# The edge counts of a tensor-product layer, with the one-hots as moving data

## The chip, the cores and the metric

The kernel runs on one core of a Trainium2 chip. The metric is the time of one execution on the device in microseconds. The core has five engines that work side by side: TensorE (matrix products, PE in the profile, its loads of weights PEld), VectorE (DVE), ScalarE (ACT), GpSimd (POOL) and SyncE (SP). Semaphores order their work against each other.

## The reference

Four graph layers run one after the other on 3125 nodes of 256 values and 100000 edges. Each layer's result is added to the nodes and normalized. The change is in the second, a tensor-product layer (`_L1_gnn_ref`). What matters of it:

```python
h = silu(edge_attr @ fc_w1 * ...)
h = silu(h @ fc_w2 * ...)
w = h @ fc_w3 * ...
wA, wB, wC, wD = split(w, 4, axis=1)
...
ns = segment_sum(mid_s, src, num_segments=N)
nv = segment_sum(mid_v, src, num_segments=N)
deg = segment_sum(ones((src.shape[0],)), src, num_segments=N)
dn = rsqrt(maximum(deg, 1.0))
ns = ns * dn[:, None]
nv = nv * dn[:, None, None]
```

So the layer sums 512 values per edge (`mid_s` and `mid_v`) at the edge's source node, counts the edges of each node (`deg`), and scales each node's sums by one over the root of its count.

## The kernel before, in words

**Order of the edges.** At its start the kernel sorts the edges by bucket, once by destination and once by source. A bucket is 128 consecutive nodes; there are NB = 26 (the last one is for padding). The sorted edges are worked on in macros of ME = 512 edges, as Q = 4 quarters of 128 edges, one edge per partition. All edges of a macro belong to one bucket. `jmap_s` has one entry per macro: its bucket j.

**One turn.** The layer has NM = 224 turns. Each engine runs its own loop over them, written out by hand for U = 4 turns (`macro_loops`), and meets the others at semaphores alone. A turn with M(0) as the macro to be summed does:
- GpSimd (`pool_a`) gathers the rows of `y` for macro M(3), SyncE (`sync_a`) loads its records.
- TensorE (`tensor`, `turn`) goes through two macros by turns. For M(2) it computes the edge weights `w`: `transposes` (L1796), `layer_1` (L1802), `layer_2` (L1809), `layer_3` (L1817). Between them it does the four quarters of `sums` (L1827, L1828) for M(0): quarter 0 after the transpose, quarter 1 after `layer_1`, quarters 2 and 3 after `layer_2`.
- ScalarE (`act`) applies silu and copies for M(2), among them L1856, which makes `layer_1`'s operand, and, first in its turn, L1866 for the macro before.
- VectorE writes the one-hots (`one_hot`) of M(3) and the messages of M(1) (`messages`), then adds the finished sums of M(0) (`add_sums`, L1911 and L1912).

**The sums.** The one-hot `oh[:, u, q, :]` of a quarter has a row per edge and a column per node of the bucket. L1828 loads it as weights (128x128, f32) and streams the 512 values of the messages through it, in two passes of the profile, into bank 5 or 6 of PSUM. L1827 loads the upper halves of the same one-hot as bf16 weights and streams one column of ones, which gives the counts of this bucket's nodes in one column, in bank 2 or 7. Both pairs of banks alternate from turn to turn, so a turn waits for the flush of two turns before. At the end of a turn L1911 adds that column to column j of `deg` in SBUF, and L1912 adds the 512 columns to `acc[:, j]`. Both read j into a register of VectorE.

**After the loop.** `scale` (VectorE) takes the larger of `deg` and 1, `root` (ScalarE) its square root, and `scale` the reciprocal. `deg` has nodes on partitions and buckets in columns.

**Names used below.** The attention layers use similar loops. In the last one (L1373 to L1429) L1400 is a bf16 matmul with 24 columns of weights (`turn_scores`), L1410 and L1413 have 128 columns of weights (`node_scores`), and L1373 reads j into a register of TensorE. In the first, L962 is a transpose to 8 rows and L989 a matmul with 128x128 weights.

Of the kernel before, what the change touches and what calls it, by code (L numbers as in the profile page):

```python
# [16 lines left out]
I32 = mybir.dt.int32  # L17
BF16 = mybir.dt.bfloat16
ALU = mybir.AluOpType
# [3 lines left out]
P = 128  # L23
# [12 lines left out]
NB = NT + 1  # L36
PAD_KEY = NB * P - 1
Q = 4
# [4 lines left out]
NMA = NM + 6  # L43
# [50 lines left out]
def top(ap):  # L94

    return ap.bitcast(BF16)[..., 1::2]
# [6 lines left out]
def gnn_kernel(nc, io, out):  # L103
    ctx = ExitStack()
    with ctx:
        def sb(name, shape, dt=F32):
            return ctx.enter_context(nc.sbuf_tensor(name, shape, dt))

        def sem(name):
            return ctx.enter_context(nc.semaphore(name))  # L110
# [17 lines left out]
        ident = sb("ident", [P, P])  # L128
        ones = sb("ones", [P, P])
# [5 lines left out]
        jmap = {"d": sb("jmap_d", [1, NMA], I32), "s": sb("jmap_s", [1, NMA], I32)}  # L135
        deg = sb("deg", [P, NB])
# [4 lines left out]
        oh = sb("oh", [P, U, Q, P])  # L141
# [3 lines left out]
        small = sb("small", [P, 640])  # L145
        wts = sb("wts", [P, 3 * 2 * D])
        rows = sb("rows", [P, 3 * D])
        by_src = sb("by_src", [P, 3, EC + EC // (NM // U)])

        ps = ctx.enter_context(nc.psum_tensor("ps", [P, 8, 512], F32))  # L150
# [4 lines left out]
        def S(name):  # L155
            if name not in sems:
                sems[name] = sem(name)
            return sems[name]

        T = nc.tensor  # L160
        V = nc.vector
# [6 lines left out]
        def vchain(e):  # L168

            the_vchain.e = e  # L170
            return the_vchain
# [4 lines left out]
        def phase(**fns):  # L176

            bars[0] += 1
            meet = 5 * bars[0]
            for name, todo in programs.items():  # L180
                todo.append((fns.get(name), meet))
# [406 lines left out]
        def both(*fns):  # L588
            return lambda e: [fn(e) for fn in fns]

        phase(sync=both(load, project0["sync"]), vector=both(place, project0["vector"]),
              tensor=both(totals, project0["tensor"]), scalar=fill_ring, gpsimd=scatter)
# [195 lines left out]
        def macro_loops(ahead, first, body, after=None, start=0, side=None):  # L788

            def go(e):
                for m in range(ahead):
                    first(e, Macro(0, m))
                if side and side[0]:
                    side[0](e)
                for m in range(start):
                    body(e, lambda lag, m=m: Macro(0, m + lag))
                with e.Fori(0, NM // U) as i:
                    for u in range(U):  # L800
                        body(e, lambda lag, i=i, u=u + start: Macro(i, u + lag))
                        if side:
                            side[1](e, i, u)
                if side and side[2]:
                    side[2](e)
                if after:
                    after(e)
            return go
# [896 lines left out]
        def layer1():  # L1705
# [36 lines left out]
            s = stages("e1", "oh", "tr", "at", "h1", "g1", "h2", "g2", "w", "wac", "wr", "msg", "sum", "flush")  # L1742
# [16 lines left out]
            msg = [big[:, u * 2048:(u + 1) * 2048].rearrange("p (q c h n) -> p q c h n", q=Q, c=4, h=2)  # L1759
                   for u in range(2)]  # L1760
            psW = ps[:, 3:5, :].rearrange("p b c -> p (b c)").rearrange("p (q k n) -> p q k n", q=Q, k=4)
            psDeg = [ps[:, 2, 0:1], ps[:, 7, 0:1]]
            acc = acc_raw[:, :, 0:2 * D]

            def sync_a(e, m):
                i = e.snap(m.index())
# [52 lines left out]
                                        start=True, stop=True)  # L1819
                last.then_inc(s["w"], 1)  # L1820

            def sums(e, m, q):
                if q == 0:
                    e.wait_ge(s["oh"], m.done())
                    e.wait_ge(s["msg"], m.done())
                    e.wait_ge(s["flush"], m.done(2))
                T.matmul(psDeg[m.v], top(oh[:, m.u, q, :]), top(ones[:, 0:1]), start=(q == 0), stop=(q == Q - 1))  # L1827
                ins = T.matmul(ps[:, 5 + m.v, :], oh[:, m.u, q, :],  # L1828
                               msg[m.v][:, q].rearrange("p c h n -> p (c h n)"),
                               start=(q == 0), stop=(q == Q - 1))  # L1830
                if q == Q - 1:
                    ins.then_inc(s["sum"], 1)

            def tensor(e):
                e.wait_ge(S("e1_fc"), 16 * (Q + 4))
                e.wait_ge(S("e1_go"), 1)
                for m in range(2):
                    for part in (transposes, layer_1, layer_2, layer_3):
                        part(e, Macro(0, m))

                def turn(e, M):

                    transposes(e, M(2))
                    sums(e, M(0), 0)
                    layer_1(e, M(2))
                    sums(e, M(0), 1)
                    layer_2(e, M(2))
                    sums(e, M(0), 2)
                    sums(e, M(0), 3)
                    layer_3(e, M(2))  # L1850
                macro_loops(0, None, turn)(e)

            def act(e, m):
                e.wait_ge(s["tr"], m.done())
# [51 lines left out]
            def add_sums(c, e, m):  # L1906
                j = e.value_load(jmap["s"][0:1, bass.ds(m.index(), 1)], min_val=0, max_val=NB - 1)
                e.wait_ge(s["flush"], m.done(1))
                e.wait_ge(s["sum"], m.done())
                dj, aj = deg[:, bass.ds(j, 1)], acc[:, bass.ds(j, 1), :]  # L1910
                V.tensor_tensor(dj, dj, psDeg[m.v], ALU.add)  # L1911
                V.tensor_tensor(aj, aj, ps[:, 5 + m.v, :], ALU.add).then_inc(s["flush"], 1)  # L1912

            def dve(e):
                c = vchain(e)
                c(V.memset(deg[:, :], 0.0))
                c(V.memset(rows[:, 0:384], 0.0))
                c.wait()
                e.sem_inc(S("e1_go"), 1)
                for m in range(2):  # L1920
                    for q in range(Q):
                        one_hot(e, Macro(0, m), q)
                cc = Chain(e, cB)
                messages(cc, e, Macro(0, 0), Macro(0, 2))
                per = cc.n
                e.wait_ge(S("zeroed"), 1)

                def turn(e, M):
                    c = Chain(e, cB)
                    c.n = per * M(1).off  # L1930
                    c.enter(M(1).i, U * per)
                    messages(c, e, M(1), M(3))
                    assert c.n - c.at == per
                    add_sums(c, e, M(0))
                macro_loops(0, None, turn)(e)

            def pool(e):
# [4 lines left out]
                  scalar=macro_loops(2, act, lambda e, M: act(e, M(2))), tensor=tensor, vector=dve)  # L1942
# [9 lines left out]

            def scale(e):
                c = vchain(e)
                c(V.tensor_scalar(deg[:, :], deg[:, :], 1.0, None, ALU.max))
                c.wait()
                e.sem_inc(s_act[0], 1)
                e.wait_ge(s_act[1], 1)
                c(V.reciprocal(dn, deg[:, :]))
                c.wait()  # L1960
# [2 lines left out]
                e.wait_ge(s_act[0], 1)  # L1963
                A.activation(deg[:, :], deg[:, :], ACT.Sqrt).then_inc(s_act[1], 1)

            phase(vector=scale, scalar=root)


            out_scale = (2 * MUL) ** -0.5 * MUL ** -0.5
# [253 lines left out]
```

## Time and profile before

| | us |
|---|---|
| median of 3 runs | 9040.61 (9038.01 to 9045.36) |
| the profiled execution | 9037.91 |
| its span in the trace | 9036.1 |
| TensorE busy with matmuls | 6249.3 (69%) |
| VectorE busy | 5729.5 (63%) |
| GpSimd busy | 6125.2 (68%) |
| ScalarE busy | 2476.3 (27%) |
| matmuls L1828, 1792 passes | 960.7 |
| gathers L1787 | 1218.7 |

The tensor-product layer's loop runs from about 3620 to 5108 us of the span. Busy time counts the records of instructions. A matmul's record contains the way through the array too, so records of neighbouring matmuls overlap, and a busy TensorE isn't one at its peak. The profile shows for each group of instructions how long the engine was idle ahead of it and what ended that. The granted clock of TensorE has two levels, 0.5 (1.2 GHz) and 1.0 (2.4 GHz); in between a stretch is a mixture. Names with q behind them (PEldq) are an engine's sequencer.

### The profile page before, as it was taken

To read this page: it belongs to the slowest core of one execution; us is meant where nothing else is said; L and a number is where in the kernel's file an instruction comes from. 1 tells how busy PE (TensorE), PEld (TensorE's weight loads), DVE (VectorE), ACT (ScalarE), POOL (GpSimd) and SP (SyncE) were. 2 spreads that over 40 slices of the span, in tenths; PEclk is the share of its full clock that TensorE was granted. 3 is DMA by queue.
4 is the path that set the end of the run, shared out by engine and by line. 5 is a ranking of instruction groups with operands and counts; after the bars stand their busy time and mean duration, and the time that the engine had idled before them with its cause. 6 is when DMAs were issued, how large, how long until landed. Compare 5 with 4: busy or idle time off the path is not lost. (4 is left out here: it accounts for less than half of the span.)

```text
span 9036.1 us, 124148 instructions
## 1 busy us (share of the span) xinstructions
PE 6249.3 (69%) x27682; PEld 3822.4 (42%) x27683; DVE 5729.5 (63%) x14736; ACT 2476.3 (27%) x7366; POOL 6125.2 (68%) x5632
## 2 busy tenths in 40 slices
PE   5100077777777775999999778888888887555554
PEld 2000044444444444444444445555555555334433
DVE  7000076666666665888888778888888887322223
ACT  0000044444444442333333223333333333000000
POOL 4777677777777774888888635555555555677772
PEclk8555577777777777999999889999999998777776
DMA  2000043333343342333233533333333344333354
GB/s 88 13 1 1 8 117 104 107 106 106 107 108 108 108 106 60 86 84 85 84 85 85 53 94 105 105 105 105 105 105 106 105 106 92 98 104 104 105 99 50
DMA packets 411759, 790.73 MB, mean 88 GB/s; under 512 B 198754, under 2 KB 228172, under 8 KB 411084
## 3 DMA queue, kind: packets, MB, share of 16 engines
q0 software_dynamic: 283584, 725.19, 31.8%
q1 hardware_dynamic: 128140, 65.15, 2.5%
q8 instruction: 13, 0.21, 0.0%
q14 instruction: 22, 0.18, 0.0%
HBM read 749.73 MB, written 40.22 MB: 87 GB/s over the span
## 5 line engine op out<-in xcount | busy, mean ns | idle before, releaser
L1787 POOL DMA_INDIRECT gat<-y,rec_sb_s x908 | 1218.7, 1342 | 276.5 <-issue 259.4
L1545 DVE TENSOR_REDUCE small<-ps 128x2 f32<-128x1024 f32 x900 | 1091.7, 1222 | 308.1 <-PE ps L1413 266.4
L907 POOL DMA_INDIRECT gat<-kv,rec_sb_d x912 | 988.3, 1084 | 302.1 <-issue 275.2
L1350 POOL DMA_INDIRECT gat<-kv,rec_sb_s x916 | 889.9, 971 | 403.6 <-issue 314.3
L2051 POOL DMA_INDIRECT gat<-x,rec_sb_d x908 | 863.1, 951 | 332.2 <-issue 265.0
L2065 PE MATMUL ps<-gat,oh 128*128 128x256 f32 x1792 | 664.4, 537 | 528.7 <-DMA gat<-x,rec_sb_d 402.5
L495 POOL DMA_INDIRECT rec_s<-wts,rows x784 | 836.5, 1067 | 238.9 <-issue 238.3
L434 POOL DMA_INDIRECT rec_d<-small x784 | 764.9, 976 | 335.2 <-issue 247.2
L1828 PE MATMUL ps<-big,oh 128*128 128x512 f32 x1792 | 960.7, 635 | 0.0
L1360 POOL TENSOR_TENSOR big<-gat,big 128x1024 f32<-128x1024 f32 x225 | 442.6, 1967 | 588.4 <-ACT big L1483 588.4
L989 PE MATMUL ps<-big,oh 128*128 128x264 f32 x1800 | 795.3, 558 | 0.4
L939 PE MATMUL ps<-qz,work 128*128 x1824 | 672.6, 533 | 145.1 <-issue 135.7
L2065 PEld LDWEIGHTS ps<-gat,oh 128*128 128x128 f32 x1792 | 458.6, 268 | 734.3 <-issue 390.0
L928 PE MATMUL ps<-work,oh 128*128 128x128 bf16 x912 | 119.6, 272 | 883.4 <-DVE oh L1096 883.2
L2085 DVE TENSOR_TENSOR acc<-acc,ps 128x256 f32 x224 | 94.3, 421 | 826.1 <-PE ps L2065 826.1
L1410 PE MATMUL ps<-wts,work 128*128 128x512 bf16 x1804 | 613.0, 425 | 0.0
L1413 PE MATMUL ps<-wts,small 128*128 128x512 bf16 x1804 | 608.9, 423 | 0.0
L1217 DVE TENSOR_TENSOR big<-ps,gat 128x1024 f32<-128x1024 f32 x226 | 276.7, 1224 | 480.9 <-DMA gat<-kv,rec_sb_d 480.3
L939 PEld LDWEIGHTS ps<-qz,work 128*128 128x128 f32 x1824 | 463.9, 267 | 248.2 <-issue 164.0
L1241 DVE MEMSET acc<- 128x6864 f32 x1 | 5.8, 5778 | 868.3 <-issue 868.3
L1040 ACT ACTIVATE work<-ps 128x512 f32<-128x512 bf16 x228 | 136.1, 597 | 1353.1 <-PE ps L928 1353.1
L928 PEld LDWEIGHTS ps<-work,oh 128*128 128x128 bf16 x912 | 84.1, 123 | 973.8 <-issue 937.4
(276 smaller groups left out, 13812.2 us busy)
## 6 DMA issues: line engine op xcount, KB each, us to landing
gat<-kv,rec_sb_s POOLq DMA_INDIRECT x916
gat<-kv,rec_sb_d POOLq DMA_INDIRECT x912
rec_sb_s<-rec_s SPq DMA_DIRECT2D x456, 32.0 KB, 1.8
gat<-y,rec_sb_s POOLq DMA_INDIRECT x908
gat<-x,rec_sb_d POOLq DMA_INDIRECT x908
kv<-big SPq DMA_DIRECT2D x52, 256.0 KB, 2.0
rec_d<-small POOLq DMA_INDIRECT x784
rec_s<-wts,rows POOLq DMA_INDIRECT x784
```

The lines of the kernel that those rows point to most:

```text
L434: e.indirect_dma_start(out=recs["d"], out_offset=bass.IndirectOffsetOnAxis(ap=pring[:, h * RH + t:h * RH + t + 1], axis=0), in_=rr[:, h, t ...
L495: e.indirect_dma_start(out=recs["s"], out_offset=bass.IndirectOffsetOnAxis(ap=pr[:, t:t + 1], axis=0), in_=rr[:, t, :], in_offset=None).th ...
L907: e.indirect_dma_start(out=gat[:, m.u, q, :], out_offset=None, in_=table, in_offset=bass.IndirectOffsetOnAxis(ap=r_sb[:, m.u, q, 0:1].bitc ...
L939: last = T.matmul(to, oht[:, m.v, q * P:(q + 1) * P], qz[:, bass.ds(j, 1), :], start=True, stop=True)
L989: last = T.matmul(psO[m.v], oh[:, m.u, q, :], pvb[:, m.v, q, :], start=(q == 0), stop=(q == Q - 1))
L1350: e.indirect_dma_start(out=gat[:, m.u, q, :], out_offset=None, in_=table, in_offset=bass.IndirectOffsetOnAxis(ap=r_sb[:, m.u, q, 0:1].bitc ...
L1410: T.matmul(to[:, n, :], bigI, nh[m.u], start=True, stop=False)
L1545: V.tensor_reduce(mx[:, 2 * pair:2 * pair + 2], psH[pair % 2], AX.X, ALU.max).then_inc(s_hr, 1)
L1787: e.indirect_dma_start(out=rows_y[m.u][:, q, :], out_offset=None, in_=y1, in_offset=bass.IndirectOffsetOnAxis(ap=r_sb[:, m.u, q, 0:1].bitc ...
L1828: ins = T.matmul(ps[:, 5 + m.v, :], oh[:, m.u, q, :], msg[m.v][:, q].rearrange("p c h n -> p (c h n)"), start=(q == 0), stop=(q == Q - 1))
L2051: e.indirect_dma_start(out=gat[:, m.u, q, 0:D], out_offset=None, in_=x3, in_offset=bass.IndirectOffsetOnAxis(ap=r_sb[:, m.u, q, 0:1].bitca ...
L2065: last = T.matmul(ps[:, 5 + m.v, 0:D], oh[:, m.u, q, :], gat[:, m.u, q, 0:D], start=(q == 0), stop=(q == Q - 1))
```

## The change

The counting matmul has its operands exchanged. `row_of` is a strip of 51 or 52 bf16 columns that are zero but for a one in column 25 (NB - 1). Its slice from column r on, 26 wide, has a one in row position 25 - r only. With the slice from j' = 25 - j as weights and the one-hot as 128 moving columns, the matmul adds the quarter's counts in row j of a 26x128 block of PSUM and zeros in the other rows. That block, in bank 2, is opened with zeros ahead of the loop, accumulates over all 224 turns, and is closed behind it. So nothing is added to `deg` in a turn. TensorE needs j' for each macro: `row_at` holds it for all of them (`V.tensor_scalar` from `jmap_s`), and each turn begins with a register load of it on TensorE (`row_start`). After the loop the block has buckets on partitions, so VectorE copies it, TensorE transposes it, and `scale` goes on from PSUM.

```diff
-            psDeg = [ps[:, 2, 0:1], ps[:, 7, 0:1]]
+            psDeg = ps[0:NB, 2, 0:P]
+            row_of = small[:, 336:362].bitcast(BF16)
             acc = acc_raw[:, :, 0:2 * D]
+            zero_row = small[:, 384:512]
+            counts = small[0:NB, 512:640]
+            row_at = by_src[0:1, 0, 0:NMA].bitcast(I32)
...
-            def sums(e, m, q):
+            def row_start(e, m):
+                return e.value_load(row_at[0:1, bass.ds(m.index(), 1)], min_val=0, max_val=NB - 1)
+
+            def sums(e, m, q, j):
...
-                T.matmul(psDeg[m.v], top(oh[:, m.u, q, :]), top(ones[:, 0:1]), start=(q == 0), stop=(q == Q - 1))
+                T.matmul(psDeg, row_of[:, bass.ds(j, NB)], top(oh[:, m.u, q, :]), start=False, stop=False)
...
+                T.matmul(psDeg, row_of[:, 0:NB], top(zero_row), start=True, stop=False)
+
                 def turn(e, M):
-
+                    j = row_start(e, M(0))
                     transposes(e, M(2))
-                    sums(e, M(0), 0)
+                    sums(e, M(0), 0, j)
...
                 macro_loops(0, None, turn)(e)
+                T.matmul(psDeg, row_of[:, 0:NB], top(zero_row), start=False, stop=True)
...
-                dj, aj = deg[:, bass.ds(j, 1)], acc[:, bass.ds(j, 1), :]
-                V.tensor_tensor(dj, dj, psDeg[m.v], ALU.add)
+                aj = acc[:, bass.ds(j, 1), :]
                 V.tensor_tensor(aj, aj, ps[:, 5 + m.v, :], ALU.add).then_inc(s["flush"], 1)
...
-                c(V.memset(deg[:, :], 0.0))
+                c(V.memset(row_of, 0.0))
+                c(V.memset(zero_row, 0.0))
                 c(V.memset(rows[:, 0:384], 0.0))
+                c.wait()
+                c(V.memset(row_of[:, NB - 1:NB], 1.0))
+                c(V.tensor_scalar(row_at, jmap["s"][:, :], -1.0, float(NB - 1), ALU.mult, ALU.add))
...
-                c(V.tensor_scalar(deg[:, :], deg[:, :], 1.0, None, ALU.max))
+                c(V.tensor_copy(counts, psDeg))
+                c.wait()
+                e.sem_inc(S("o1_counts"), 1)
+                e.wait_ge(S("o1_turned"), 1)
+                c(V.tensor_scalar(deg[:, :], ps[:, 0, 0:NB], 1.0, None, ALU.max))
...
+            def turn_counts(e):
+                e.wait_ge(S("o1_counts"), 1)
+                T.transpose(ps[:, 0, 0:NB], counts, ident[0:NB, 0:NB]).then_inc(S("o1_turned"), 1)
+
+            phase(vector=scale, scalar=root, tensor=turn_counts)
```

On TensorE, one turn of the layer's loop, before: the transpose, the quarters of the sums and the layers of M(2). A row's last number pair is the output (rows of the array x columns that move).

```order
L1796 MATMUL ps<-ident,rec_sb_s 64x128 [waits e1_rec3,e1_g2]
L1826 REGISTER_ALU [waits e1_msg,e1_oh]
L1827 MATMUL ps<-ones,oh 128x1 [waits e1_flush]
L1828 MATMUL ps<-big,oh 128x512
L1799 REGISTER_ALU
L1802 MATMUL ps<-work,rows 128x128 [waits e1_g1,e1_at]
L1802 MATMUL ps<-work,rows 128x128
L1827 MATMUL ps<-ones,oh 128x1
L1828 MATMUL ps<-big,oh 128x512
L1809 MATMUL ps<-work,rows 128x256 [waits e1_g1,e1_g2]
```

The same place after (L1796, L1802, L1809, L1827, L1828 have become L1800, L1806, L1813, L1834, L1835):

```order
L1827 ISA
L1827 TENSOR_LOAD by_src
L1827 ISA x2
L1800 MATMUL ps<-ident,rec_sb_s 64x128 [waits e1_rec3,e1_g2]
L1833 REGISTER_ALU [waits e1_msg,e1_oh]
L1834 ISA [waits e1_flush]
L1834 MATMUL ps<-oh,small 26x128
L1835 MATMUL ps<-big,oh 128x512
L1803 REGISTER_ALU
L1806 MATMUL ps<-work,rows 128x128 [waits e1_g1,e1_at]
L1806 MATMUL ps<-work,rows 128x128
L1834 MATMUL ps<-oh,small 26x128
```

No matmul has moved: each counting matmul stands where it stood, with 26 rows and 128 columns in place of 128 rows and one column. New are the register load with its three register operations ahead of the turn, and one register operation ahead of the first counting matmul, which now carries the wait for the flush.

On VectorE, the end of a turn, before:

```order
L1907 ISA
L1907 TENSOR_LOAD jmap_s
L1907 ISA x2
L1911 ISA [waits e1_sum,e1_flush]
L1911 TENSOR_TENSOR deg<-deg,ps 128x1
L1912 ISA
L1912 TENSOR_TENSOR acc<-acc,ps 128x512
```

and after:

```order
L1917 ISA
L1917 TENSOR_LOAD jmap_s
L1917 ISA x2
L1921 ISA [waits e1_sum,e1_flush]
L1921 TENSOR_TENSOR acc<-acc,ps 128x512
```

One operation of one column and its register operation are gone; the wait for the sums now stands ahead of the addition of 512 columns.

The last attention loop isn't changed. On TensorE its register load of j (L1373) stands in the program as follows:

```order
L1410 MATMUL ps<-wts,work 128x512 [waits a2_hr,a2_sp]
L1410 MATMUL ps<-wts,work 128x512
L1413 MATMUL ps<-wts,small 128x512 x2
L1410 MATMUL ps<-wts,work 128x512 [waits a2_hr]
L1410 MATMUL ps<-wts,work 128x512
L1413 MATMUL ps<-wts,small 128x512 x2
L1373 TENSOR_LOAD jmap_s
L1373 ISA x2
```

The load is the last of these in the program and stands there before and after alike.

## Rows read from the trace of the kernel before

**Rows 1.** The page, busy us (share of the span) and instructions of each engine.
```profile
PE 6249.3 (69%) x27682; PEld 3822.4 (42%) x27683; DVE 5729.5 (63%) x14736; ACT 2476.3 (27%) x7366; POOL 6125.2 (68%) x5632
```
**Rows 2.** Table by stretches: us, busy PE, PEld, DVE, ACT, POOL, clock, DMA share, GB/s.
```profile
4300.00:4600.00 300.00, 291.67 (x1231) 142.46 (x1231) 267.11 (x638) 93.38 (x320) 244.53 (x183) 1.00 0.30 84
```
**Rows 3.** Waits, 3700 to 5000 us: waiting line, releaser, us in total, times, longest.
```profile
PE ps L1802 <- ACT work L1856: 35.7, 197, 0.2
DVE deg L1911 <- PE ps L1828: 142.0, 196, 0.8
```
**Rows 4.** Timeline of one turn: start, us, engine, line, operation, output and inputs.
```profile
4307.67 0.30 PE L1796 MATMUL ps<-ident,rec_sb_s 128*64 128x128 f32 x1
4307.81 0.17 PE L1827 MATMUL ps<-ones,oh 128*128 128x1 bf16 x1
4307.84 1.10 PE L1828 MATMUL ps<-big,oh 128*128 128x512 f32 x2
...
4308.80 0.27 ACT L1856 ACTIVATE work<-ps 64x128 f32<-64x128 f32 x1
...
4309.12 0.71 PE L1802 MATMUL ps<-work,rows 64*128 64x128 f32 x4 [0.18 <-ACT work L1856]
...
4311.84 0.94 DVE L1903 TENSOR_TENSOR big<-work,rec_sb_s 128x768 f32<-128x768 f32 x1
```
**Rows 5.** Single lines: durations in ns (min/median/max), first and last start.
```profile
L1827 PE MATMUL ps<-ones,oh x788: 166/167/179, 3700.4 to 4998.8; 128*128 128x1 bf16 x197
...
L1828 PE MATMUL ps<-big,oh x1576: 592/634/677, 3700.4 to 4999.3; 128*128 128x512 f32 x197
...
L1802 PE MATMUL ps<-work,rows x788: 271/272/374, 3701.7 to 4996.2; 64*128 64x128 f32 x197
...
L1400 PE MATMUL ps<-work,small x904: 218/219/228, 5328.1 to 7629.0; 128*24 128x128 bf16 x181
...
L1911 DVE TENSOR_TENSOR deg<-deg,ps x224: 139/155/156, 3633.4 to 5107.3; 128x1 f32 x112
```
**Rows 6.** Timeline, TensorE, from quarter 2 to quarter 3 of the sums.
```profile
4311.18 0.17 PE L1827 MATMUL ps<-ones,oh 128*128 128x1 bf16 x1
...
4312.15 0.17 PE L1827 MATMUL ps<-ones,oh 128*128 128x1 bf16 x1
4312.17 0.68 PE L1828 MATMUL ps<-big,oh 128*128 128x512 f32 x1
```
**Rows 7.** Timeline, TensorE, last attention loop, around L1400.
```profile
5600.93 0.38 PE L1413 MATMUL ps<-wts,small 128*128 128x512 bf16 x1
5601.24 0.39 PE L1400 MATMUL ps<-work,small 128*24 128x128 bf16 x4
5601.57 0.39 PE L1410 MATMUL ps<-wts,work 128*128 128x512 bf16 x1
```
**Rows 8.** Timeline, TensorE, from L1802 to quarter 1 of the sums.
```profile
4316.16 0.27 PE L1802 MATMUL ps<-work,rows 64*128 64x128 f32 x1
4316.36 0.18 PE L1827 MATMUL ps<-ones,oh 128*128 128x1 bf16 x1
```
**Rows 9.** Timeline, TensorE, first attention loop, around L962.
```profile
1173.90 0.27 PE L962 MATMUL ps<-ident,small 128*8 128x128 f32 x1 [1.06 <-DVE small L1150]
1174.01 0.45 PE L989 MATMUL ps<-big,oh 128*128 128x264 f32 x1
```
**Rows 10.** Line L1373 on TensorE's sequencer, 5646.5 to 5647.4 us.
```profile
L1373 PEldq TENSOR_LOAD <-jmap_s x1: 297/297/297, 5646.6 to 5646.6; - x1
L1373 PEldq SEQ_ASSERT  x1: 18/18/18, 5647.2 to 5647.2; - x1
```
**Rows 11.** Timeline, TensorE, the same stretch.
```profile
5647.31 0.63 PE L1413 MATMUL ps<-wts,small 128*128 128x512 bf16 x1
```
**Rows 12.** Line L1794 on TensorE's sequencer, 4310 to 4318 us.
```profile
L1794 PEldq FUSED_REGOPS  x1: 43/43/43, 4312.5 to 4312.5; - x1
```
**Rows 13.** Timeline, TensorE, the transpose behind L1794.
```profile
4314.27 0.30 PE L1796 MATMUL ps<-ident,rec_sb_s 128*64 128x128 f32 x1
```

More of the change, by code:

```diff
@@ L1839, in tensor @@
                         part(e, Macro(0, m))
+                T.matmul(psDeg, row_of[:, 0:NB], top(zero_row), start=True, stop=False)
                 def turn(e, M):
+                    j = row_start(e, M(0))
                     transposes(e, M(2))
-                    sums(e, M(0), 0)
+                    sums(e, M(0), 0, j)
                     layer_1(e, M(2))
-                    sums(e, M(0), 1)
+                    sums(e, M(0), 1, j)
                     layer_2(e, M(2))
-                    sums(e, M(0), 2)
-                    sums(e, M(0), 3)
+                    sums(e, M(0), 2, j)
+                    sums(e, M(0), 3, j)
                     layer_3(e, M(2))
                 macro_loops(0, None, turn)(e)
+                T.matmul(psDeg, row_of[:, 0:NB], top(zero_row), start=False, stop=True)
             def act(e, m):
@@ L1964, in root @@
                 A.activation(deg[:, :], deg[:, :], ACT.Sqrt).then_inc(s_act[1], 1)
-            phase(vector=scale, scalar=root)
+            def turn_counts(e):
+                e.wait_ge(S("o1_counts"), 1)
+                T.transpose(ps[:, 0, 0:NB], counts, ident[0:NB, 0:NB]).then_inc(S("o1_turned"), 1)
+            phase(vector=scale, scalar=root, tensor=turn_counts)
             out_scale = (2 * MUL) ** -0.5 * MUL ** -0.5
```

## The prediction

> **What bounds the kernel now.** Start with the page's busy shares [rows 1]. No engine is full over the whole span (TensorE 69%, VectorE 63%), so a share of the span decides nothing. The change touches only the tensor-product layer, so take the table by stretches there [rows 2]: in 300 us of it TensorE has 291.7 us of matmuls, VectorE 267, GpSimd 245, ScalarE 93, at the full granted clock (1.00, which is 2.4 GHz). The table of waits counts 197 turns in 1300 us [rows 3], so a turn takes 6.60 us.
>
> Which wait ends last is read from the same table [rows 3]. TensorE waits for another engine at one line only, L1802 for ScalarE's L1856, 35.7 us in 197 turns, 0.18 us each. VectorE waits for TensorE's sums ahead of L1911, 142.0 us in 196 turns, 0.72 us each: it is early. So a turn is two pieces, and the timeline of one turn shows them [rows 4]. Once the turn before has done its L1817, ScalarE makes the four copies of L1866 and then L1856, until 4309.07, and TensorE beside it does L1796 and the first quarter of the sums (L1827, L1828), then waits. From L1802 at 4309.12 to the end of L1817 TensorE runs alone and decides. A cost on TensorE counts in full in the second piece (quarters 1, 2 and 3 of the sums), and in the first (quarter 0) only beyond its slack.
>
> **What a pair costs today.** A record of a matmul contains its pipeline as well: L1827 streams one column and takes 0.166 us, so a stream is the duration less 0.166. A 512-column pass of L1828 takes at least 0.592, which makes 0.426 us of stream [rows 5]. In quarter 2 one L1827 starts at 4311.18 and the next at 4312.15 [rows 6]: 0.97 us, less two passes (0.852) leaves 0.118. That is all that counting costs per quarter, and it is not L1827's stream. The weights of L1827 are loaded under the matmul before it; those of L1828 (128 columns, f32) can go in only once L1827 has started, and one column hides none of it: the first pass reads 0.68 in place of 0.59.
>
> **Part 1, operands exchanged: 26 rows out, 128 columns moving.** By the same rows this would be nothing: the 128 columns stream for 0.218 - 0.166 = 0.052 us (L1400, the same shape but for 24 rows [rows 5]), and L1828's load of 0.118 now runs beside them. But the timeline of the last attention loop [rows 7] shows what stands around a narrow output. L1413 (128x128) starts its last pass at 5600.93 with 0.38: its stream ends at 5601.14, and L1400, 128x24, starts at 5601.24. Its fourth matmul starts 0.219 before the group's end of 5601.63, at 5601.41, has streamed at 5601.46, and L1410 (128x128 again) starts at 5601.57. Neither gap is bridged by a load that was fetched early. So 0.10 us in and 0.10 us out.  The same step stands where the number of rows of the array changes, in this layer: L1802 (64 rows) starts its last matmul at 4316.16 with 0.27, its stream ends at 4316.27, and L1827 (128 rows) starts at 4316.36 [rows 8].
>
> Against it speak two narrow outputs that cost nothing: L962 (8 columns of weights) starts at 1173.90, streams 0.105, and L989 follows at 1174.01; and L1796 (64 columns) is followed by L1827 after 0.14, its stream 0.105 as well [rows 4, 5, 9]. Both are f32 transposes. The new line is a plain bf16 matmul of 128 columns like L1400, so I price it by L1400.
>
> The Trainium skill, TensorEngine Tiling (Array Packing), Key Properties, says that a change of tiling mode, not of the tile alone, drains TensorE; its Restrictions say that f32 transposes can't use column tiling. By that rule narrow plain matmuls pay and the two transposes don't, and the rows agree. The same page's Instruction Overhead says that a free size of 1 costs as much as 60, by which the exchange would be nearly free (128 against 60 columns); the sum by that alone would be the first rival's.
>
> The sum for a quarter, new less old: 0.10 in, 0.01 for the 26-column load, which no longer hides (the longest L1400, a first one, reads 0.228, the median 0.219 [rows 5]), 0.05 stream, 0.10 out, then L1828's load as before.
> - Quarters 2 and 3: 0.25 us each.
> - Quarter 1: L1827 comes from L1802's 64 rows and pays the way in already, so 0.05 + 0.10 less rounding, 0.145 us.
> - Quarter 0: 0.25, against its slack. Its second pass [rows 4] ends at 4308.94 (4307.84 + 1.10), its stream at 4308.77, a change of rows makes 4308.87, and L1802 starts at 4309.12: 0.25 us of slack. It just fits; I take 0.00 and keep 0.05 for the range. The cover is ScalarE's chain; without it quarter 0 costs 0.25 as well.
>
> 0.25 + 0.25 + 0.145 = 0.65 us per turn, and 224 turns (the count of L1911 [rows 5]) make **146 us**. The turn becomes 7.25 us.
>
> **Part 2, the bucket is read on TensorE.** Each turn now has a register load on TensorE's sequencer. In the last attention loop the same sequence (register operation, load, register operation, assertion) has its load at 5646.6 and its assertion at 5647.2 [rows 10], with the operation ahead 0.7 us. It stands in the program behind four L1413, and runs before L1413 starts at 5647.31: the sequencer reads it while the array has a queue in front of it [rows 10, 11]. In this layer the sequencer is at L1794 at 4312.5, and the transpose that follows it starts at 4314.27 [rows 12, 13], 1.7 us ahead. 0.7 fits, so zero. Bounds: 0 to 0.7 us a turn, nearest row zero. The weight address in a register is prepared once a turn (one more register operation), also ahead.
>
> **Part 3, VectorE.** L1911 goes, 0.155 us a turn [rows 5]. VectorE idles 0.72 us right before it, waiting for the sums [rows 3]; it will idle longer. The sums wait for the flush of two turns before, since the two banks alternate, and that is long done. Zero; bounds -0.155 to 0. GpSimd's gathers and the record loads have more time per turn.
>
> **Part 4, the ends.** Ahead of the loop two memsets and one operation of 230 elements; behind it a copy of 26 rows, a transpose on TensorE (as L1796, 0.30 [rows 4]), and two hand-overs ahead of the square root on ScalarE. With three small VectorE operations of L1911's size, a transpose and two hand-overs (L1856 ends at 4309.07, L1802 starts at 4309.12, so 0.05 to 0.3 each) I estimate 1.5 us, between 0.5 and 3.
>
> Sum: 146 + 1.5 = 147 us on the profiled execution of 9037.9 (span 9036.1); the median of the runs is 2.7 above it, so 9040.6 + 147 = **9188 us**, 1.6% slower.
>
> **Rivals.**
> - *No change of mode.* If the 26-row form behaves like L962 and L1796, the load of L1828 hides the stream, and only the ends remain: 9042. For it: two rows of 0.00 to 0.03. Against: all of L1400. 8%.
> - *One side only.* If just the way out costs, quarters 1 to 3 pay 0.145 each, 0.44 x 224 = 97: 9139. If just the way in, quarters 2 and 3 pay 0.10 each, 45: 9087. [rows 7] show both sides; 3%.
> - *The load isn't hidden.* The load waits for the array, or the lead of 1.7 us has shrunk below 0.7: 0.7 x 224 = 157 more, 9345. [rows 10, 11] speak against it. 3%.
> - *The clock falls.* TensorE streams less densely; if part of the layer went to 1.2 GHz, 10% at that level would add at least 0.1 x 7.25 x 224 = 162: 9350. Its matmuls still cover nearly the whole turn, and the layer held 1.00 throughout [rows 2]. 3%.
> - *Faster: VectorE ends the turn.* If L1911 lay on the path (sums ready, L1911, L1912, the next messages, the next sums), its 0.155 x 224 = 35 us would be saved: 9006. It decides once VectorE's idle time before L1911 is zero; it is 0.72, and the messages end at 4312.78 (L1903, 4311.84 + 0.94) for sums that come behind the transpose of 4314.27 [rows 4, 13]. 3%.
>
> **How the numbers follow.** The forecast has the other 80%. Within it, steps of 0.08 to 0.12 us in place of 0.10 and 0.05 for quarter 0 make 0.55 to 0.78 us a turn, 9165 to 9217. The range is 9125 to 9245: the lower end takes in the way out alone, the upper one quarter 0 wholly uncovered (0.90 x 224 = 202, 9244). Outside stay the first rival, the way in alone, the faster case and the two of over 9300, just under 2 in 10. A measurement here tells about 0.2%, 18 us, from no change. Faster: 3%. Same: the first rival, 8%. Slower: 89%.
>
> **What the profile after would show.** Turns of 7.25 us, 1624 for the 224. The matmuls that count: 128x26, 128 columns, 0.22 us. From such a quarter's start to the next (quarter 2 to 3) 1.22 in place of 0.97, the previous pass's stream ending 0.10 before the narrow matmul starts, and L1828 starting 0.15 after it rather than 0.02 to 0.03. L1802 waits about 0.00 for L1856 where it waited 0.18. VectorE's wait for the sums grows from 0.72 to about 1.5 (0.65 + 0.13). The register load starts over a microsecond before its matmuls. GpSimd shows no new wait. Wrong would be: L1828 within 0.03 of the narrow matmul (no drain out); no gap ahead of it (none in); a register load after which the array stands empty; a granted clock below 1.00 in the layer.

## The result, and the profile after

| kernel | median | runs, lowest to highest | profiled execution: span | granted clock, mean |
|---|---|---|---|---|
| before | 9039.31 us | 9034.71 to 9045.36 (4) | 9036.1 us | 0.809 |
| after | 9178.47 us | 9175.69 to 9180.6 (4) | 9175.9 us | 0.811 |

The changed kernel takes 1.0153 of the time of before (95% interval 1.0136 to 1.0171), 139 us more. Forecast were 147 us more, and slower.

The page of after, as [rows 1]: TensorE has 180 us more of busy time, VectorE 23 us less. The added busy time is not the added time: a record of a matmul holds its pipeline as well, and part of it lay beside a wait.

```profile
PE 6429.0 (70%) x27685; PEld 3847.8 (42%) x27686; DVE 5706.4 (62%) x14516; ACT 2478.4 (27%) x7366; POOL 6262.3 (68%) x5632
```

The same 300 us as [rows 2], of after; the columns are those of [rows 2]. TensorE's records now cover all of the stretch (291.67 before), and VectorE has 30 us less in it, since fewer turns fit in and L1911 is gone. The clock stays at 1.00.

```profile
4300.00:4600.00 300.00, 300.00 (x1122) 134.43 (x1121) 237.57 (x538) 85.42 (x292) 249.42 (x167) 1.00 0.27 77
```

The waits of after from 3700 to 5000 us, as [rows 3] (waiting engine, line, releaser; us in total, times, longest). Lines have moved: L1802 is now L1806, L1809 L1813, L1817 L1821, L1827 L1834, L1828 L1835, L1856 L1866, L1912 L1921, and L1911 is gone.

```profile
DVE acc L1921 <- PE ps L1835: 268.4, 180, 1.6
...
PEld ps L1806 <- ACT work L1866: 138.6, 180, 0.8
```

180 turns where 197 stood. TensorE's matmul wait for ScalarE (35.7 us before) has no row any more; the row that is left is the weight load's, for the same L1866. VectorE waits 268.4 / 180 = 1.49 us for the sums, 0.72 before. So the order of who waits for whom is that of before, and TensorE is late by more.

One turn of after on TensorE (start, us, line, operation, output and inputs), as [rows 4, 6 and 8]:

```profile
4301.04 1.14 PE L1821 MATMUL ps<-rows,work 64*128 64x256 f32 x8
4302.10 0.30 PE L1800 MATMUL ps<-ident,rec_sb_s 128*64 128x128 f32 x1
4302.34 0.23 PE L1834 MATMUL ps<-oh,small 128*26 128x128 bf16 x1
4302.50 1.12 PE L1835 MATMUL ps<-big,oh 128*128 128x512 f32 x2
4303.56 0.71 PE L1806 MATMUL ps<-work,rows 64*128 64x128 f32 x4
4304.20 0.23 PE L1834 MATMUL ps<-oh,small 128*26 128x128 bf16 x1
4304.36 1.12 PE L1835 MATMUL ps<-big,oh 128*128 128x512 f32 x2
4305.32 0.59 PE L1813 MATMUL ps<-work,rows 128*128 128x256 f32 x2
4305.85 0.23 PE L1834 MATMUL ps<-oh,small 128*26 128x128 bf16 x1
4306.00 1.13 PE L1835 MATMUL ps<-big,oh 128*128 128x512 f32 x2
4307.06 0.23 PE L1834 MATMUL ps<-oh,small 128*26 128x128 bf16 x1
4307.22 1.13 PE L1835 MATMUL ps<-big,oh 128*128 128x512 f32 x2
4308.28 1.13 PE L1821 MATMUL ps<-rows,work 64*128 64x256 f32 x8
```

From L1821 to L1821 it is 7.24 us, 6.60 before. From quarter 2 (4305.85) to quarter 3 (4307.06) it is 1.21, 0.97 before. L1835 starts 0.16 behind the narrow matmul; L1828 stood 0.02 behind L1827 [rows 6]. L1806 follows quarter 0 without an idle time; L1802 waited 0.18 [rows 4]. ScalarE's operand for it comes at the same moment:

```profile
4303.24 0.27 ACT L1866 ACTIVATE work<-ps 64x128 f32<-64x128 f32 x1
```

It ends at 4303.51, 0.05 ahead of L1806, the distance that stood before too (4309.07 and 4309.12). From the transpose to L1806 it is 1.46 us, 1.45 before: quarter 0 has used up its slack and no more.

**Where the 139.8 us of the span went**, by the starts of the same lines in the two traces:
- ahead of the layer: 1.9 us (its memset of `rows` starts at 3604.22 in place of 3602.29);
- from there to the third `layer_2` (L1813, L1809 before), called the third turn here and below (two macros are computed ahead of the loop, so it lies in the loop's first turn): 7.2 us (35.64 in place of 28.42);
- the 223 turns behind it: 1613.07 in place of 1473.48, 139.6 us. The steady turn is 7.233 in place of 6.602, 0.631 more, and 223 times that is 140.7; 1.1 us come back since the last turns of before were themselves slower (6.65 to 7.19);
- from the last turn to the attention loop behind the layer: 6.7 us less;
- the rest: 2.2 us less.

**The start** is the place where the change costs more than it was priced at. The timelines of all engines at the layer's start, after and then before:

```profile
3603.96 11.19 POOL L1951 MEMSET acc<- 128x13312 f32 x1 [8.58 <-SPq L2180]
...
3604.64 10.64 DVE L1930 TENSOR_SCALAR by_src<-jmap_s 1x230 int32<-1x230 int32 x1
3604.66 0.06 DVE L1929 MEMSET small<- 128x1 bf16 x1
3615.41 1.34 SPq L1780 DMA_DIRECT2D rows<-in_L_gnn_fc_w  x4
```

```profile
3602.18 11.19 POOL L1938 MEMSET acc<- 128x13312 f32 x1 [8.58 <-SPq L2159]
...
3602.81 1.34 SPq L1776 DMA_DIRECT2D rows<-in_L_gnn_fc_w  x4
...
3608.62 6.08 DVE L1873 TENSOR_SCALAR oh<-iota,rec_sb_s 128x128 f32<-128x128 f32 x8 [5.95 <-DMA rec_sb_s<-rec_s]
```

The new operation of 230 elements on VectorE, L1930, takes 10.64 us. It ends at 3615.28, and GpSimd's memset of `acc` at 3615.15 (3603.96 + 11.19). SyncE issues the layer's first loads only behind it, 10.7 us later than before (12.6 less the 1.9). The first `layer_2` (L1813) comes 20.05 us after the memset of `rows`, 9.24 before. Two of the expectations below call this the first sums; the first sums themselves (L1835, L1828) come at 31.88 us, 24.60 before. The second turn gives 3.6 of the 10.8 back (8.68 us long, 12.27 before).

**The end.** VectorE's first operation behind the layer comes 10.1 us after the last turn's L1813 (14.1 before), so 4.0 are gained at the barrier, where GpSimd comes last with its gathers; the counts' way through TensorE costs 0.8, as the timeline of after shows: 5263.05 to 5266.12 is 3.07 us, and before, from 5118.32 to 5120.59, it was 2.27.

```profile
5263.05 0.28 DVE L1968 COPY small<-ps 26x128 f32<-26x128 f32 x1 [6.21 <-SPq L2180]
...
5263.54 0.27 PE L1985 MATMUL ps<-ident,small 26*128 26x26 f32 x1 [6.37 <-DVEq L1970]
5263.84 0.19 DVE L1972 TENSOR_SCALAR deg<-ps 128x26 f32<-128x26 f32 x1 [0.51 <-PE ps L1985]
...
5266.12 0.34 SPq L631 DMA_DIRECT2D wts<-in_L_gnn_w_s  x1
```

What the barrier takes goes with the turn's length: in the traces of the experiments below this distance is 10.2 to 14.8 us where the turn is 6.36 to 6.61, 11.9 at 7.07, and 5.3 to 5.4 in the three others at 7.23 (a9, e3, e4), in which no gather is left behind the last turn. That GpSimd is less far behind in a slower loop is read from this, not tested.

3.2 us more go with the clock: the projection behind it is the same work in 56.49 us in place of 59.74, at a granted clock of 0.80 in place of 0.76 (table by stretches, before and then after). What made the clock higher there is open, and it is not shown to come from the change: in the repeat of after (a9) the same stretch has 58.87 us at 0.76, in e3 and e4, with the same turn, 62.28 at 0.72 and 63.51 at 0.69.

```profile
5120.59:5180.33 59.74, 40.82 (x312) 40.13 (x312) 22.75 (x133) 15.52 (x26) 26.94 (x26) 0.76 0.01 2
```

```profile
5266.12:5322.61 56.49, 37.27 (x312) 36.58 (x312) 22.75 (x133) 15.53 (x27) 26.96 (x26) 0.80 0.01 3
```

### The profile page after: what moved, and what is told of

Its sections match the earlier page's. It is cut to its first block and busy times, and to the rows that moved or that the text cites. A ratio compares the mean times of both kernels' runs of the same rounds, so it can differ in the third digit from the quotient of the medians.

```text
span 9175.9 us, 124832 instructions
## 1 busy us (share of the span) xinstructions
PE 6429.0 (70%) x27685; PEld 3847.8 (42%) x27686; DVE 5706.4 (62%) x14516; ACT 2478.4 (27%) x7366; POOL 6262.3 (68%) x5632
## 5 line engine op out<-in xcount | busy, mean ns | idle before, releaser
L1791 POOL DMA_INDIRECT gat<-y,rec_sb_s x908 | 1358.2, 1496 | 283.4 <-issue 260.8
L1835 PE MATMUL ps<-big,oh 128*128 128x512 f32 x1792 | 1009.3, 645 | 0.0
```

Of the source, the lines that this page charges most:

```text
L1791: e.indirect_dma_start(out=rows_y[m.u][:, q, :], out_offset=None, in_=y1, in_offset=bass.IndirectOffsetOnAxis(ap=r_sb[:, m.u, q, 0:1].bitc ...
L1835: ins = T.matmul(ps[:, 5 + m.v, :], oh[:, m.u, q, :], msg[m.v][:, q].rearrange("p c h n -> p (c h n)"), start=(q == 0), stop=(q == Q - 1))
```

## The experiments

They ran on chips on which before takes 9927 to 9931 us: other layers are longer there, this one's turns are not (the changed kernel, run again beside e5, e7 and e8, has 7.233 us there too; before itself has no trace there). So times are compared as ratios, and the turn is read from each trace: the median distance of the same matmul in the 224 turns. Several executions there have two to four long turns at the layer's start, up to 18.6 us, in which some waits are put down to no recorded instruction; they come in e3, e4, e7 and the repeats and not in e1 (which has three near its end), e2, e5, e8, and I don't explain them. The steady turn does not depend on them.

| run | what it is | steady turn | ratio to before (95%) |
|---|---|---|---|
| before | 128x128 weights, 1 column, 4 a turn | 6.602 us | |
| after | 128x26 weights, 128 columns, 4 | 7.233 us | 1.0153 (1.0136 to 1.0171) |
| a9_after_again | the same, on another chip | 7.233 us | 1.0136 (1.0110 to 1.0162) |
| e1_wide_rows | 128x128, 128 columns, 4 | 6.602 us | 1.0010 (0.9995 to 1.0025) |
| e1_again | the same | 6.606 us | 1.0013 (0.9996 to 1.0031) |
| e2_narrow_old | 128x26, 1 column, 4 | 7.071 us | 1.0083 (1.0057 to 1.0109) |
| e3_no_register_load | after, no register | 7.227 us | 1.0128 (1.0102 to 1.0155) |
| e4_row_at_early | after, L1930 early | 7.234 us | 1.0136 (1.0110 to 1.0163) |
| e6_wide_early | e1 and e4 | 6.606 us | 1.0001 (0.9987 to 1.0014) |
| e5_no_count | no counting | 6.361 us | 0.9952 (0.9935 to 0.9968) |
| e7_one_wide_512 | 128x128, 512 columns, 1 | 6.362 us | 0.9958 (0.9941 to 0.9974) |
| e7_again | the same | 6.358 us | 0.9956 (0.9935 to 0.9978) |
| e8_one_narrow_512 | 128x26, 512 columns, 1 | 6.520 us | 0.9988 (0.9974 to 1.0001) |

**The theory**: what costs is the change of the array's form, from 128 columns of weights to 26 and back. **The rivals**: the added stream of 128 columns, the register load, or one way of the change alone.

### Only the width undone

```diff
-            psDeg = ps[0:NB, 2, 0:P]
+            psDeg = ps[:, 2, 0:P]
...
-                T.matmul(psDeg, row_of[:, bass.ds(j, NB)], top(oh[:, m.u, q, :]), start=False, stop=False)
+                T.matmul(psDeg, row_of[:, bass.ds(j, P)], top(oh[:, m.u, q, :]), start=False, stop=False)
```

> The changed kernel with one edit: the strip has 153 columns, and its slice is 128 wide in place of 26, so the counting matmul writes 128 rows (102 of them zeros) and TensorE keeps its full width. The stream of 128 columns, the register load and the slow start stay. Theory one, TensorE stops for 0.10 us each time its width changes: both stops go, the turn falls from 7.24 back to about 6.60 us (quarter 2 to quarter 3 0.97 us), and the time to about 9178 - 0.635 x 224 = 9036, plus some of the slow start: 9036 to 9052, ratio to before 1.000 to 1.001. Rival, the exchanged operands themselves cost it (128 strided columns moving, or weights addressed by a register): the turn stays at 7.2 us and the time at 9178. Rival, narrow weights were a gain that the wide ones lose: above 9178.

Measured: 6.602 us. The whole change is in this kernel (operands exchanged, 128 moving columns, register load, no L1911), and the turn is that of before to the third decimal. Its timeline on TensorE, quarters 2 and 3:

```profile
5002.09 0.59 PE L1813 MATMUL ps<-work,rows 128*128 128x256 f32 x2
5002.52 0.22 PE L1834 MATMUL ps<-oh,small 128*128 128x128 bf16 x1
5002.58 1.07 PE L1835 MATMUL ps<-big,oh 128*128 128x512 f32 x2
5003.49 0.22 PE L1834 MATMUL ps<-oh,small 128*128 128x128 bf16 x1
...
5007.07 0.71 PE L1806 MATMUL ps<-work,rows 64*128 64x128 f32 x4 [0.18 <-ACT work L1866]
```

The narrow matmul of after started 0.53 behind L1813 (4305.85 after 4305.32), the wide one starts 0.43 behind it; L1835 follows 0.06 later and not 0.16. Quarter to quarter it is 0.97, as before, though 128 columns stream in place of one: L1835's load runs beside them. The 0.18 us of waiting for ScalarE are back. This excludes the stream, the register load and all else that both kernels have as a cause of the 0.63 us by itself. Beside narrow weights the stream does cost, as the next run shows.

### Only the width done

```diff
-                T.matmul(psDeg[m.v], top(oh[:, m.u, q, :]), top(ones[:, 0:1]), ...)
+                T.matmul(psDeg[m.v][0:NB], top(oh[:, m.u, q, 0:NB]), top(ones[:, 0:1]), ...)
```

> The kernel before with one edit: L1827 takes only the first 26 columns of the one-hot as weights, so it writes 26 rows, and L1911 adds 26 rows. It leaves out the counts of nodes 26 to 127 of each bucket. One column still moves, no register is read, nothing else differs. Theory one (change of width): quarters 2 and 3 pay 0.10 in, 0.01 for the load and 0.10 out, 0.21 each less rounding, quarter 1 0.09, quarter 0 is covered: 0.49 to 0.51 us a turn, 110 to 114 us, 9149 to 9153, ratio 1.012. Rival (exchange itself): no change, 9039.

Measured: 7.071 us, 0.469 more than before, a little under the 0.49 to 0.51 expected. The same two quarters:

```profile
5002.44 0.59 PE L1809 MATMUL ps<-work,rows 128*128 128x256 f32 x2
5002.96 0.18 PE L1827 MATMUL ps<-ones,oh 128*26 128x1 bf16 x1
5003.07 1.12 PE L1828 MATMUL ps<-big,oh 128*128 128x512 f32 x2
5004.13 0.18 PE L1827 MATMUL ps<-ones,oh 128*26 128x1 bf16 x1
```

In: 0.52 behind L1809 (0.43 in e1). Out: 0.11 from L1827 to L1828 (0.02 in before), one column long. On the path lie two ways in (quarters 2 and 3) and three ways out (quarters 1 to 3): 0.469 / 5 = 0.094 us for each. Both ways cost, and with a single moving column. What separates this kernel from after on TensorE's path is the stream, and its size fits: 7.233 - 7.071 = 0.162, three times 0.054. The ratio of the whole time, 1.0083, missed the 1.012 expected; 224 turns of 0.469 us are 105 us of 9931, 1.0106, inside the interval. No width between 26 and 128 was tried.

### The register load

```diff
 def row_start(e, m):
-    return e.value_load(row_at[0:1, bass.ds(m.index(), 1)], min_val=0, max_val=NB - 1)
+    return None
...
-  row_of[:, bass.ds(j, NB)]
+  row_of[:, 0:NB]
```

> The changed kernel without the register load in each turn: the weights are always the slice from column 0, so all counts go to the last row. It leaves out which bucket a count belongs to. Theory one (the load runs ahead of the array): nothing changes, 9174 to 9182. Rival (the load or the address in a register is on the path): up to 0.7 us a turn less, and if it were the cause of the whole loss, 9039.

Measured: 7.227 us for the turn, 0.006 less; 224 turns make 1.3 us, below what the ratio can tell. The trace of after has the load on TensorE's sequencer at 4306.5, 2.8 us ahead of the transpose at 4309.34 that opens its turn (the line's one load in 4306 to 4307 us; name, ns, start):

```profile
L1827 PEldq TENSOR_LOAD <-by_src x1: 299/299/299, 4306.5 to 4306.5; - x1
```

### The operation beside GpSimd's memset

```diff
                 V.memset(wts[:, 0:4 * P], 0.0).then_inc(w_zero, 1)
-                e.wait_ge(w_zero, 1)
+                V.tensor_scalar(by_src[0:1, 0, 0:NMA].bitcast(I32), jmap["s"][:, :], -1.0, float(NB - 1),
+                                ALU.mult, ALU.add).then_inc(w_zero, 1)
+                e.wait_ge(w_zero, 2)
...
-                c(V.tensor_scalar(row_at, jmap["s"][:, :], -1.0, float(NB - 1), ALU.mult, ALU.add))
```

> The changed kernel with the 230 row numbers computed one phase earlier, beside the clearing of the layer's weights, where GpSimd has no memset. In the changed kernel this operation took 10.64 us beside GpSimd's memset of 11.19 us and held back the loads of the layer's weights. Theory, the wait is for GpSimd's memset: it takes under 0.5 us there, the first turn begins 10 us earlier, and 5 to 11 us of it reach the end (the loop's first turns can take up some): 9167 to 9173. Rival, the operation is slow by itself (integers on one partition): it takes 10 us there too, and nothing is gained: 9178.

The operation's half came in: the same 230 elements, issued ahead of the layer where GpSimd has no memset, take 204 ns.

```profile
L1736 DVE TENSOR_SCALAR by_src<-jmap_s x1: 204/204/204, 4257.4 to 4257.4; 1x230 int32<-1x230 int32 x1
```

The first `layer_2` comes at 9.44 us in place of 20. The time's half missed: 1.0136, the ratio that after has in its repeat (a9, on another chip with the same time of before). This execution has long turns of 7.6, 13.0 and 11.2 us right behind its start, as that repeat does (10.2, 9.5 and 10.5), so it could not say what the start is worth. I ran the pair again without the narrow form:

> The changed kernel with two differences: the counting matmul writes 128 rows, the weights padded with zero columns (as in e1_wide_rows), and the row starts are computed ahead of the layer, where no GpSimd memset runs beside the operation (as in e4_row_at_early). It computes the whole result. Theory (the 10.64 us that VectorE's operation of 230 elements took stood beside GpSimd's memset, and held the layer's start by 10.8 us less the 3.6 us that the second turn gives back): the operation reads about 0.20 us, the first sums of the layer come 9.4 to 9.5 us after the memset in place of 20.1, the steady turn stays 6.60, and the layer ends 6 to 8 us earlier than in e1_wide_rows. Rival (the layer's start is bound by the gathers and the record loads, so what VectorE does there is covered): the first sums come early, the turns behind them are longer, and the layer ends as in e1_wide_rows, within 1 us.

> e1_wide_rows once more, beside e6_wide_early on one chip, as its partner. Both theories: steady turn 6.60 us, the operation of 230 elements 10.6 us, first sums 20.1 us after the memset, and the time of the kernel before within 0.2%. If the three long turns near the end of the layer that e1_wide_rows showed (9.2, 11.7 and 8.4 us) come from this kernel, they stand here again at the same place; if they are a disturbance of that execution, they don't.

e6 has almost no long turns at its start (one of 7.27), and the first run of e1 none. Up to the third turn none has come yet in any of the three: it starts at 28.32 us in e6, at 35.09 in e1 and at 35.13 in e1's repeat on e6's chip, 6.8 us apart, as before and after were (28.42 and 35.64, 7.2). The rest of the layer can't be compared so closely: e6's ends 13.8 us ahead of e1's and 21.8 ahead of the repeat's, with the long turns in it, where 6 to 8 were expected of the first. So the stall costs some 7 us of the start; that it costs them of the whole time is carried by the traces alone, since the ratios, 1.0001 and 1.0013, have intervals that overlap. The repeat of e1 has its own long turns (8.6, 10.7, 14.6 and 7.8 us, right behind the start), at other places than the first run's three (9.2, 11.7 and 8.4 us, turns 209 to 211), so those belong to the executions and not to the kernel.

The timeline of e4 at the layer's start shows that the stall is one of VectorE's `tensor_scalar` beside this memset, not of L1930 alone:

```profile
4307.60 11.19 POOL L1952 MEMSET acc<- 128x13312 f32 x1 [8.59 <-SPq L2181]
...
4308.30 0.06 DVE L1931 MEMSET small<- 128x1 bf16 x1
...
4314.38 4.55 DVE L1885 TENSOR_SCALAR oh<-iota,rec_sb_s 128x128 f32<-128x128 f32 x2 [6.02 <-DMA rec_sb_s<-rec_s]
```

With L1930 out of the way, the first pair of one-hots takes 4.55 us, and ends at 4318.93; the memset ends at 4318.79. In before the same line has 6.08 us for its first eight, where after, with the memset over, has 1.66. In all three the held operations end 0.08 to 0.15 us behind the memset, while VectorE's own small memsets pass beside it (0.06 us). The Trainium skill, SBUF — State Buffer, Who interferes with whom, says that VectorE and GpSimd share a pair of ports which the first one to issue holds for its whole instruction, the other being blocked, and that `tensor_scalar` can take that pair. By that rule L1930 waits for the end of the memset; the trace agrees (10.64 us beside it, 0.204 without).

### What counting costs at all, and one matmul for it

e5, the kernel before without its counting matmuls:

> The kernel before without L1827, and with ones added to the counts in its place. It leaves out the counting of edges. It measures what a counting matmul costs before: theory (one column hides none of L1828's load): quarters 2 and 3 0.115 each, quarter 1 0.02, quarter 0 nothing: a turn of 6.35 us, 56 us less than before, ratio 0.994. Rival (the short matmul was free, a row of 0.17 us that overlaps): 6.60 us and no change.

e7, the wide form, one counting matmul a turn over all four quarters' one-hots (with the row numbers made early, as in e4, and the matmuls that open and close the block widened to 512 columns):

```diff
-                T.matmul(psDeg, row_of[:, bass.ds(j, P)], top(oh[:, m.u, q, :]), start=False, stop=False)
+                if q == 0:
+                    T.matmul(psDeg, row_of[:, bass.ds(j, P)], top(oh[:, m.u, :, :].rearrange("p q c -> p (q c)")),
+                             start=False, stop=False)
...
-                c(V.tensor_copy(counts, psDeg[0:NB]))
+                c(V.tensor_reduce(counts, psDeg[0:NB].rearrange("p (q c) -> p c q", q=Q), AX.X, ALU.add))
```

> A design from what the first four runs showed: the exchanged operands let one matmul count a whole macro. Weights are the 128 wide slice, and all four one-hots move at once (512 columns) in quarter 0's place, into four blocks of one bank, added after the loop; the row numbers are made early. Theory: no change of width, so no stop; L1835 in quarters 2 and 3 loses the 0.115 us in which its weights followed a short matmul, quarter 1 0.02 (0.129 less 0.11), and quarter 0 pays 0.10 more, inside its slack of 0.25. The turn becomes 6.60 - 0.25 = 6.35 us, and the time 56 us less than before: 8983 by the first chip's 9039, ratio 0.994. Rival, ScalarE or VectorE or the gathers take over as the bound (VectorE had 0.72 us of idle time, GpSimd's gathers wait in it): 6.60 remains, ratio 1.000. Rival, the 512 columns don't fit in quarter 0's slack: 6.45 to 6.5.

> As the run with one wide matmul of 512 columns, but with the 26 wide slice, so TensorE's width changes twice in a turn rather than eight times. Theory: quarter 0 pays 0.10 + 0.01 + 0.21 + 0.10 in addition, less slack 0.25, that is 0.17 us more than the wide one: a turn of 6.52 us, 18 us less than before (ratio 0.998), 38 us more than the wide one. Rival (no stops, or stops that hide): the same as the wide one.

Measured: e5 6.361, e7 6.362, e8 6.520 us a turn. e7 counts at no cost that the turn shows. Its timeline:

```profile
5005.40 0.30 PE L1802 MATMUL ps<-ident,rec_sb_s 128*64 128x128 f32 x1
5005.53 0.39 PE L1837 MATMUL ps<-oh,small 128*128 128x512 bf16 x1
5005.76 1.02 PE L1839 MATMUL ps<-big,oh 128*128 128x512 f32 x2
5006.85 0.71 PE L1808 MATMUL ps<-work,rows 64*128 64x128 f32 x4
5007.49 1.12 PE L1839 MATMUL ps<-big,oh 128*128 128x512 f32 x2
```

The 512 columns stream in the 0.2 to 0.3 us in which TensorE would wait for ScalarE anyway (a wait that no longer shows), and quarters 1, 2 and 3 run without a counting matmul. Before, counting cost 6.602 - 6.361 = 0.241 us a turn. Against e1, the four passes of quarters 2 and 3 save 0.23 of it (1.81 us in e7, 5002.52 to 4.33, and 2.04 in e1, 5002.52 to 4.56); quarter 1 saves 0.02, as the sums there follow L1802's 64 rows and, as the prediction priced it, a load is exposed there with or without counting.

```profile
5002.52 1.88 PE L1839 MATMUL ps<-big,oh 128*128 128x512 f32 x4
5004.33 1.13 PE L1823 MATMUL ps<-rows,work 64*128 64x256 f32 x8
```

e8 pays one way in and one out for its 26 rows, of which the slack takes part: 0.158. It is still faster a turn than before, by 0.08; the whole time doesn't show it, since its interval (0.9974 to 1.0001) takes in 1.

> e7_one_wide_512 once more: one counting matmul of 512 columns per turn with 128 rows out, the row starts computed early. It computes the whole result. Theory (the time is gained by 0.24 us in each of some 212 turns, and the last dozen turns are held at about 7.1 us by the gathers): 6.36 us for the steady turn, the last turns about 7.1 us with VectorE waiting for gathered rows, ratio 0.994 to 0.998. Rival (the slow last turns were a disturbance of that execution): the last turns read 6.36 too, and the layer is another 8 to 10 us shorter.

e7 beats both kernels on each of two occasions: 0.9958 and 0.9956, by the medians 50 and 40 us below before, where 56 (0.994) were expected. 0.240 x 224 is 54 us; where the rest stays is half settled. The long turns at the start hold the most in the two profiled executions: four of 8.1 to 10.2 us in the first, 11.5 us above the steady turn together, and two of 18.6 and 8.9 in the second, 14.8 us. Besides, the last five turns in the first run take 6.78 to 7.45 us, 3.9 us together. The waits there, 5730 to 5765 us, have VectorE waiting for gathered rows, and the table by stretches shows the DMA engines at 0.91 from 5734 to 5765 where they are at 0.44 in 5400 to 5700, with fewer GB/s:

```profile
DVE gat L1899 <- DMA gat<-y,rec_sb_s: 7.3, 5, 2.0
```

```profile
5400.00:5700.00 300.00, 296.62 (x1132) 148.15 (x1130) 271.46 (x615) 97.52 (x334) 240.37 (x188) 1.00 0.44 86
5734.00:5765.00 31.00, 27.71 (x102) 13.55 (x100) 25.09 (x58) 8.60 (x29) 22.96 (x17) 1.00 0.91 79
```

The last turns of before, e5 and e8 are slow in the same way, those of after, with 7.23 us a turn, are not. In the second run of e7 the DMA share rises again, to 0.87, but only two turns are long (8.06 and 7.36): of the two ways expected, the last dozen slow or none, neither came in whole. A high DMA share alone doesn't slow a turn (e1 has 0.93 there, 5760 to 5810 us, and turns of 6.60). So the gathers are close to being the bound at the layer's end at 6.4 us a turn; why they need more of the DMA engines there for the same bytes is open.

## Why the prediction was right, step by step

- **What bounds the turn**: right. TensorE from L1802 to L1817, with 0.18 us of slack in quarter 0. All costs in quarters 1 to 3 came in full, and VectorE's wait grew to 1.49 (forecast about 1.5).
- **Which rows price a narrow matmul**: right, L1400 and not the two f32 transposes. The rival "no change of mode" fell with e2, "one side only" with the timelines of after and e2, which show both sides. The Trainium skill's rule quoted there (TensorEngine Tiling (Array Packing), Key Properties), that a change of tiling mode drains TensorE, agrees with the runs: 26 columns of bf16 pay 0.094 a change (e2), while L1800, a 64-column transpose in f32, is still followed by a wide matmul after 0.14 (e1). The runs show the gap and its size; that it is a drain is that page's word.
- **The terms of a turn**: forecast 0.10 + 0.10 for a change in and out, 0.05 for the stream, 0.01 for the small load, 0.65 in all; measured 0.094 for each of the five changes and 0.054 for each of the three streams, 0.631. The load's 0.01 is inside these.
- **Quarter 0 at nothing**: right, and to the last hundredth. The 0.25 us fill the slack: L1806 follows L1835 without idle time, 1.46 us behind the transpose where it was 1.45.
- **The register load at nothing**: right. 0.006 us a turn, with a lead of 2.8 us where 1.7 was read.
- **VectorE's saved operation at nothing**: right. e1 has it saved too, and 6.602.
- **The ends at 1.5 us**: this is the term that was mis-sized, in both directions. I priced L1930 as a small operation of L1911's size (0.155 us). It took 10.64, and the start became 7.2 us longer; the row that would have warned stands in the trace of before, L1873 beside the same memset at 6.08 us for eight, and I had not read it. The end, forecast as longer, was 6.7 shorter: the counts cost 0.8, the barrier gave back 4.0, and a higher clock, which other executions with this loop don't have, 3.2. The two errors almost cancel, so part of the closeness of the total (139 and 147) is luck; without them the turns alone give 139.6 to 140.7.
- **147 forecast, 139.8 in the trace**: of the 7.3 us between them 224 x (0.65 - 0.631) = 4.3 are the turn's, 0.6 one turn that the trace counts in the start, 1.1 the slower last turns of before, and 1.3 the ends (1.5 forecast; 1.9 + 7.2 - 6.7 - 2.2 = 0.2 measured).
- The clock stayed at 1.00 in the layer, and no new wait appeared on GpSimd.

## What to carry to other kernels

Count the changes of the weights' width on TensorE's path, not the columns: padding 26 weight columns with zeros to 128 cost no time here and took back the whole 0.63 us a turn, and small matmuls are best gathered into one of 512 columns at a place where the engine waits anyway. Price a new matmul by a row of the same type and width, since f32 transposes of 8 and 64 columns behaved otherwise than bf16 matmuls of 24 and 26. Before a small VectorE operation is put at a kernel's seam, look at what GpSimd does there: beside its memset of 11 us, 0.2 us became 10.6.

## What I had not expected of the hardware

- A `tensor_scalar` of 230 int32 elements on one partition takes 0.204 us alone and 10.64 beside a GpSimd memset that only writes; VectorE's own memsets pass beside it in 0.06 us.
- A matmul of one column costs the load of the next one: 0.115 us in each of quarters 2 and 3. 128 moving columns (0.052 us) in its place are free, as the load then runs beside them: e1 and before have the same turn.
- The projection behind the layer, unchanged, took 59.74 us at a granted clock of 0.76 and 56.49 at 0.80, and up to 63.51 at 0.69 in e4. So a few us of an execution's time hang on the clock of a stretch that the change doesn't touch.
